# Weighing the values of two query tiles in one run of TensorE

## What is computed

```python
def attention(h, wq, wk, wv, wo):
    q = (h @ wq).reshape(b, s, NH, D).transpose(0, 2, 1, 3)
    k = (h @ wk).reshape(b, s, NKV, D).transpose(0, 2, 1, 3)
    v = (h @ wv).reshape(b, s, NKV, D).transpose(0, 2, 1, 3)
    k = jnp.repeat(k, GROUPS, axis=1)
    v = jnp.repeat(v, GROUPS, axis=1)
    scores = jnp.einsum('bhqd,bhkd->bhqk', q, k) / jnp.sqrt(jnp.float32(D))
    scores = jnp.where(causal, scores, jnp.finfo(scores.dtype).min)
    attn = jax.nn.softmax(scores, axis=-1)
    out = jnp.einsum('bhqk,bhkd->bhqd', attn, v)
    return out.transpose(0, 2, 1, 3).reshape(b, s, NH * D) @ wo
```

## Time and profile before

| | us |
|---|---|
| three runs: lowest, median, highest | 1846.94, 1847.69, 1847.88 |
| the profiled execution, own time | 1847.24 |
| its span, first to last instruction | 1845.5 |
| busy in the span: PE, PE's weight loads | 1745.3, 1388.8 |
| busy in the span: ACT, DVE, POOL | 1061.6, 1037.0, 208.0 |
| first and last record of the runs of line 1300 | 223.9, 1343.1 |

### The profile page before, as it was taken

How to read it: one execution, slowest core, us unless ns; L and a number is a source line. 1 busy time by engine, 2 the same in 40 slices (tenths; PEclk the granted TensorE clock), 3 DMA queues, 4 the chain that set the end, 5 groups by cost and what they waited for, 6 DMA issues and landing times.

```text
span 1845.5 us, 31643 instructions
## 1 busy us (share of the span) xinstructions
PE 1745.3 (95%) x12158; PEld 1388.8 (75%) x12158; DVE 1037.0 (56%) x2595; ACT 1061.6 (58%) x2377; POOL 208.0 (11%) x236
## 2 busy tenths in 40 slices
PE   5999699999999999999999999999958999999993
PEld 4777377777777777777777777777748999999993
DVE  3677586686686677676776776766752111111112
ACT  3444487787777777777877777777731222222223
POOL 2222100000000000000000000000002222222222
PEclk9999799999999999999999999999968999999997
DMA  3000100000000000000000000000034153113443
GB/s 86 2 2 2 46 1 10 1 1 10 1 1 9 1 1 9 1 1 9 1 1 9 1 1 1 1 1 23 1 135 163 28 159 91 24 28 91 146 106 97
DMA packets 46054, 60.19 MB, mean 33 GB/s; under 512 B 8944, under 2 KB 39536, under 8 KB 45936
## 3 DMA queue, kind: packets, MB, share of 16 engines
q1 hardware_dynamic: 36336, 46.16, 7.5%
q0 software_dynamic: 7536, 10.36, 3.4%
q10 hardware_dynamic: 2064, 2.10, 0.4%
HBM read 138.43 MB, written 11.40 MB: 81 GB/s over the span
## 4 chain that ended last, share of the span: by engine, by line
PE 93%; DVE 3%; ACT 1%; POOL 1%; DMA 1%; issue 0%; SPq 0%; POOLq 0%; DVEq 0%
PE wide L1388 15%; PE bank L1300 14%; PE bank L1288 14%; PE bank L1245 9%; PE wide L1277 9%; PE wide L1278 8%; PE bank L1397 7%; PE bank L1309 6%; PE bank L1108 3%; PE wide L1120 1%; PE bank L1190 1%; PE bank L1179 1%; PE bank L1133 1%; PE bank L1235 1%; PE wide L1349 1%; PE bank L1102 1%
## 5 line engine op out<-in xcount | busy, mean ns | idle before, releaser
L886 DVE CUSTOM_DVE_ANT_0 arena<-wide,arena 128x896 f32<-128x896 f32 (+7 forms) x512 | 383.1, 756 | 243.0 <-PE wide L1278 236.7
L655 ACT ACTIVATE arena<-arena,nmax 128x896 f32<-128x896 f32 (+7 forms) x512 | 399.1, 780 | 89.8 <-DVE nmax L886 87.6
L662 ACT COPY arena<-bank 128x512 f32<-128x512 f32 x576 | 311.7, 586 | 82.7 <-PE bank L1288 77.2
L1277 PE MATMUL wide<-khi,qhl 128*128 128x512 f32 (+3 forms) x768 | 344.4, 450 | 1.7 <-DVE qhl L879 1.7
L1288 PE MATMUL bank<-ident,arena 128*128 128x128 f32 x2304 | 309.5, 274 | 2.5 <-DVE arena L894 1.2
L1388 PEld LDWEIGHTS wide<-wo,arena 128*128 128x128 f32 x2496 | 284.8, 192 | 3.1 <-issue 1.1
L1388 PE MATMUL wide<-wo,arena 128*128 128x128 f32 x2496 | 285.1, 275 | 0.9 <-ACT wo L710 0.9
L1288 PEld LDWEIGHTS bank<-ident,arena 128*128 128x128 f32 x2304 | 260.0, 141 | 29.3 <-issue 14.1
L1300 PE MATMUL bank<-arena,vt 128*64 128x256 f32 x2304 | 277.0, 385 | 0.0
L894 DVE TENSOR_SCALAR arena<-arena,rinv 128x896 f32<-128x896 f32 (+7 forms) x512 | 258.2, 525 | 9.1
L1049 DVE TENSOR_TENSOR wo<-wide,wo 128x512 f32<-128x512 f32 x78 | 53.9, 692 | 365.7 <-PE wide L1388 365.7
(11 more groups left out here) (221 smaller groups left out, 1576.4 us busy)
## 6 DMA issues: line engine op xcount, KB each, us to landing
arena<-in_L_ffn_w SPq DMA_DIRECT2D x117, 1024.0 KB
x_all<-in_L_attn_x ACTq DMA_DIRECT2D x1, 2048.0 KB, 9.9
wq_g<-in_L_ffn_wq SPq DMA_DIRECT2D x8, 256.0 KB, 3.0
wo<-in_L_ffn_wo SPq DMA_DIRECT2D x16, 128.0 KB, 3.0
hbuf<-acc SPq DMA_DIRECT2D x2, 1024.0 KB, 4.5
tbuf<-rT_all SPq DMA_DIRECT2D x4, 512.0 KB, 3.0
acc<-hbuf SPq DMA_DIRECT2D x4, 512.0 KB, 5.8
out<-x_all SPq DMA_DIRECT2D x8, 256.0 KB, 2.1
```

Source lines behind the costliest of these rows:

```text
L655: nc.scalar.activation(probs[t % 2][:, h, 0:w], probs[t % 2][:, h, 0:w], ACT.Exp, bias=nmax[:, t % 2, h:h + 1], scale=-1.0, accum_out=rsum ...
L662: nc.scalar.copy(pT[t % 2][m], bank_of((t, m))).then_inc(S("pT_ready"), 1)
L886: nc.vector.tensor_tensor_reduce(out=probs[t % 2][:, h, 0:w], in0=score_bank(t, h)[:, 0:w], in1=causal[:, SEQ - w:SEQ], scale=-1.0, scalar ...
L1277: mm(dst, q, khi[:, lo:lo + cols], start=True, stop=False)
```

## The change

PE weighs two tiles in one run in the even steps: in step t the tiles t - 3 and t - 2, each into its own half of `bank[2]` (512 columns now). In the next, odd step both outputs are projected right behind S0, into one of the three shared banks, for which `("O", s)` joins the list of turns, ahead of the step's blocks. ACT copies both tiles at once into an `oT` of twice the size. DVE adds both at once in the odd step, between maximum 1 and maximum 2 (in two instructions where the tiles belong to two sequences). `acc_done` counts those adds, and the loop has two more steps at its end.

```diff
+def weighed_in(t):
+    return [x for x in (t - 3, t - 2) if 0 <= x < TILES] if t % 2 == 0 else []
+def added(t):
+    return sum(len({x // TB for x in weighed_in(s) if x <= t}) for s in range(2, t + 4, 2))
+STEPS = TILES + 4
+def turns_of(t):
+    turning = 1 <= t <= TILES
+    blocks = [[(t - 1, m) for m in third(t - 1, p)] if turning else [] for p in range(3)]
+    out = [("O", t - 1)] if weighed_in(t - 1) else []
+    item = [item_of(t)] if t < TILES and item_of(t) else []
+    return out + blocks[0] + blocks[1] + blocks[2] + item
+TURNS = FIRST_ITEMS + [x for t in range(STEPS) for x in turns_of(t)]
...
-        oT = sb("oT", [P, 2, P])
+        oT = sb("oT", [P, 2, 2, P])
...
-            sp.wait_ge(S("acc_done"), BATCH * NKV * TB - TB)
+            sp.wait_ge(S("acc_done"), added(TILES - TB - 1))
...
-                if weighing:
-                    act.wait_ge(S("o2_psum"), t - 1)
-                    nc.scalar.copy(oT[:], bank[2][:, 0:2 * P].rearrange("p (j c) -> p j c", j=2)).then_inc(S("oT_ready"), 1)
+                if weighed_in(t):
+                    n = 2 * P * len(weighed_in(t))
+                    act.wait_ge(S("o2_psum"), t // 2)
+                    nc.scalar.copy(oT[:].rearrange("p x j c -> p (x j c)")[:, 0:n], bank[2][:, 0:n]).then_inc(S("oT_ready"), 1)
...
                 if scored:
                     maximum(t, 1)
+                if weighed_in(t - 1):
+                    tiles = weighed_in(t - 1)
+                    v.wait_ge(S("proj2"), (t - 1) // 2)
+                    new = bank_of(("O", t - 1))[:, 0:D * len(tiles)].rearrange("p (x d) -> p x d", d=D)
+                    for n in sorted({x // TB for x in tiles}):
+                        xs_ = [x for x in tiles if x // TB == n]
+                        at, lo = xs_[0] % (BATCH * TB), tiles.index(xs_[0])
+                        old = acc[:, at:at + len(xs_)]
+                        nc.vector.tensor_tensor(old, new[:, lo:lo + len(xs_)], old, ALU.add).then_inc(S("acc_done"), 1)
                 if scored:
                     maximum(t, 2)
                     normalise(t, 0)
-                if weighing:
-                    n, ct = divmod(t - 2, TB)
-                    v.wait_ge(S("proj2"), t - 1)
-                    at = acc[:, n % BATCH * TB + ct]
-                    nc.vector.tensor_tensor(at, bank[2][:, 2 * P:2 * P + D], at, ALU.add).then_inc(S("acc_done"), 1)
...
                     before = TURNS[TURN_OF[what] - 3]
                     if len(before) == 3:
                         wait_taken(before)
+                    elif before[0] == "O":
+                        pe.wait_ge(S("acc_done"), added(weighed_in(before[1])[-1]))
                     else:
                         pe.wait_ge(S("pT_ready"), blocks_before(before[0]) + before[1] + 1)
...
-            def values(t):
-                n, ct = divmod(t, TB)
-                if t:
-                    pe.wait_ge(S("acc_done"), t)
-                for m in range(ct + 1):
+            def values(s):
+                if s > 2:
+                    pe.wait_ge(S("oT_ready"), s // 2 - 1)
+                for x, t in enumerate(weighed_in(s)):
+                    n, ct = divmod(t, TB)
+                    for m in range(ct + 1):
...
-            def project_out(t):
+            def project_out(s):
+                wait_bank(("O", s))
+                to = bank_of(("O", s))
...
+                pe.wait_ge(S("oT_ready"), s // 2)
+                for x, t in enumerate(weighed_in(s)):
+                    for j in range(2):
+                        ins = mm(to[:, x * D:(x + 1) * D], oT[:, x, j], wo2[:, t // (BATCH * TB), j], start=(j == 0), stop=(j == 1))
...
-                if weighing:
-                    values(t - 2)
+                if weighed_in(t):
+                    values(t)
+                if weighed_in(t - 1):
+                    project_out(t - 1)
...
-                if weighing:
-                    project_out(t - 2)
```

More of the change, by code:

```diff
@@ L73, in third @@
     return range(blocks * p // 3, blocks * (p + 1) // 3)
-FIRST_ITEMS = [(0, 0, 0), (0, 1, 0), (0, 2, 0), (0, "V", 0)]
-TURNS = FIRST_ITEMS + [x for t in range(TILES + 1)
-                       for x in ([(t - 1, m) for p in range(3) for m in third(t - 1, p)] if t else []) + ([item_of(t)] if t < TILES and item_of(t) else [])]
+def weighed_in(t):
[3 more added lines that the diff above has]
+STEPS = TILES + 4
+FIRST_ITEMS = [(0, 0, 0), (0, 1, 0), (0, 2, 0), (0, "V", 0)]
+def turns_of(t):
[5 more added lines that the diff above has]
+TURNS = FIRST_ITEMS + [x for t in range(STEPS) for x in turns_of(t)]
 TURN_OF = {x: i for i, x in enumerate(TURNS)}
@@ L363, in _ @@
             t_v = tbuf.rearrange("(t p) d -> p t d", p=P)
-            sp.wait_ge(S("acc_done"), BATCH * NKV * TB - TB)
+            sp.wait_ge(S("acc_done"), added(TILES - TB - 1))
             sp.dma_start(h_v[:, 0:TB], acc[:, 0:TB]).then_inc(S("h_stored"), 16)
-            sp.wait_ge(S("acc_done"), BATCH * NKV * TB)
+            sp.wait_ge(S("acc_done"), added(TILES - 1))
             sp.dma_start(h_v[:, TB:NT], acc[:, TB:NT]).then_inc(S("h_stored"), 16)
@@ L667, in _ @@
                 evacuate(item)
-            for t in range(TILES + 2):
-                scored, turning, weighing = t < TILES, 1 <= t <= TILES, t >= 2
+            for t in range(STEPS):
+                scored, turning = t < TILES, 1 <= t <= TILES
                 if t and t <= TILES and item_of(t - 1):
@@ L688, in _ @@
                     exponent(t, 3)
-            act.wait_ge(S("acc_done"), BATCH * NKV * TB)
+            act.wait_ge(S("acc_done"), added(TILES - 1))
             for t in range(NT // 4):
@@ L925, in _ @@
                     normalise(t, 1)
-            v.wait_ge(S("acc_done"), BATCH * NKV * TB)
+            v.wait_ge(S("acc_done"), added(TILES - 1))
             for t in range(NT // 4):
@@ L1289, in turn_part @@
                     ins.then_inc(S("pT_psum"), 1)
-            def values(t):
-                n, ct = divmod(t, TB)
-                if t:
-                    pe.wait_ge(S("acc_done"), t)
-                for m in range(ct + 1):
[L1296 to L1301, removed]
+            def values(s):
[4 more added lines that the diff above has]
+                    for m in range(ct + 1):
+                        pe.wait_ge(S("pT_ready"), blocks_before(t) + m + 1)
+                        if m == ct and ct % (TB // 2) == 0:
+                            pe.wait_ge(S("v2_ready"), 2 * n + 1 + ct // (TB // 2))
+                        for u in range(2):
+                            ins = mm(bank[2][u * DH:(u + 1) * DH, x * 2 * P:(x + 1) * 2 * P], vt[:, n % 2, m], pT[t % 2][m][:, u * 2 * P:(u + 1) * 2 * P],
+                                     start=(m == 0), stop=(m == ct))
                 ins.then_inc(S("o2_psum"), 1)
-            def project_out(t):
-                if t == 0:
+            def project_out(s):
+                wait_bank(("O", s))
+                to = bank_of(("O", s))
+                if s == 2:
                     pe.wait_ge(S("wo2_loaded"), 16 * 2 * NKV)
-                pe.wait_ge(S("oT_ready"), t + 1)
-                for j in range(2):
-                    ins = mm(bank[2][:, 2 * P:2 * P + D], oT[:, j], wo2[:, t // (BATCH * TB), j], start=(j == 0), stop=(j == 1))
+                pe.wait_ge(S("oT_ready"), s // 2)
+                for x, t in enumerate(weighed_in(s)):
+                    for j in range(2):
+                        ins = mm(to[:, x * D:(x + 1) * D], oT[:, x, j], wo2[:, t // (BATCH * TB), j], start=(j == 0), stop=(j == 1))
                 ins.then_inc(S("proj2"), 1)
@@ L1335, in _ @@
                     project(item_of(t))
-            pe.wait_ge(S("acc_done"), BATCH * NKV * TB)
+            pe.wait_ge(S("acc_done"), added(TILES - 1))
             for t in range(NT // 4):
```

## The result

The changed kernel takes **1872.91 us** (median of four runs, 1872.56 to 1875.33), beside 1847.79 for the kernel before in the same comparison: 1.0135 times as long, interval 1.0122 to 1.0148. The forecast was 1875 in a range of 1860 to 1888, slower with a chance of 0.87. The profiled execution is the longest of the four, 1875.33 with a span of 1873.3.

A forecast was written before the change was run, and what follows sets the result against it. PE's in-order work was taken to bound the kernel. Fewer runs (-22.0), old waits gone (-15.5) and new waits (+65) make +27.5 us on the profiled 1847.24, forecast 1875, range 1860 to 1888.

The forecast's parts named there:

- Fewer runs, -22.0: PE's weighing: 128 runs become 65, each of the 63 saved worth 0.35 us beyond its blocks, -22.0 us.
- The cost goes with the form of the weights: On PE, a run's 0.35 us comes from 64-column weights in place of 128, not from the change of data type.
- rival C: Any full-precision matmul between scores costs the 0.35, so odd steps' output projections cancel the saving: 1897 us, 5 in 100.
- The waits that come, +65: Short odd steps and step 0 of eight: PE waits for DVE and ACT, 4.29 us per sequence, +65 us.
- 1.4 and 0.9 that went: Per sequence of eight tiles, the forecast period loses 1.4 us for fewer runs and 0.9 for present waits.
- the walk: Instruction-by-instruction timing of odd steps on PE, DVE and ACT; the last of each eight waits 2.15 us, ending at 10.12.
- the restart: On PE, a turned block that waited for DVE ends 0.77 us after DVE's end, against 0.44 alone.
- The joined add: On DVE, one add over 512 columns takes 0.69 us, like a copy; 0.84 would give 7 us more at most.
- The ends: Fifteen sequences have the new waits, 64 us, the last lacks most of them; 1 us is added for the loop's ends.
- three bounds: Margins on the sum: add 7 us more, restarts 5 less, entry into output projection 4 more; range 1868 to 1884.
- Rivals A and B: New waits overlap, 1825 to 1810 us (7 in 100); or b1 and b2 hardly wait, 1844 to 1851 (5 in 100).
- 37 us of savings: On PE over the whole loop: -22.0 us from fewer runs and -15.5 us from present waits that go.

The follow-up runs named there:

- e1: Kernel before, each weighing run of two or more blocks cut in two, second half behind the second head's score (240 runs, not 128): 1879.73 us, ratio 1.0162.
- e2: Changed kernel, with the output projection written into bank[2] instead of taking a turn of the shared banks: 1853.71 us, ratio 1.0023.
- e7: e2, with DVE making the item's low part behind maximum 1 in the last step of each eight: 1849.12 us, ratio 1.0007.
- e3: Changed kernel, each tile weighed in its own step again (128 runs), output, copy and add still paired, shared bank kept: 1867.01 us, ratio 1.0091.
- e6: e2, with single-tile runs in steps 7 and 0 of eight, pairs in 2, 4, 6 (81 runs), output projection moved: 1835.48 us, ratio 0.9934.
- e9: e6, with the item projected ahead of the turned block in step 1 of each eight: 1821.45 us, ratio 0.986.
- e4: Changed kernel with parities swapped, pairs weighed in odd steps and outputs projected in even ones: 1895.62 us, ratio 1.0252.

## Why the prediction was right

*Fewer runs, -22.0.* The size held: the trace has the 65 runs, a run has 0.15 in front, and a score of 512 columns behind it takes 0.43, in the new trace as in the old. Where that score is shorter it takes less (0.26 in ct 0), but again 0.20 more than the next one. e1 pays 0.35 per added run where a score follows and 0.30 where a block does.

*The cost goes with the form of the weights.* O between S0 and S1 leaves the next score as short as ever, so rival C is out. But 64 columns are not the whole of it: X, whose weights have 64 rows and 128 columns, also stands ahead of a score that takes 0.43 (here in ct 3), as it did before the change. So the price seems to come with any change of the form of the weights, which no run tests by itself.

```profile
741.22 0.39 PE bank L1263 x4
741.61 0.43 PE wide L1305
```

The Trainium skill's rule that a change of the tiling mode drains the engine (TensorEngine Tiling (Array Packing), Key Properties) fits what the rows show, and they give the size that it lacks: 0.15 going in, 0.15 to 0.20 coming out.

*The waits that come, +65.* The mechanism and its places were right, each with its releaser; the size was a tenth too large for a sequence. With the 1.4 and 0.9 that went, a period of 72.28 leaves 3.87 of new waits instead of 4.29. In ct 7 DVE was where the walk had it to 0.02: low part done 4.07 behind S0 (forecast 4.09), the add 5.95 (5.96). What was too long was the restart. The block behind the add ends 0.71 after it, not 0.77, and X ends 0.50 behind the copy of b4, not 0.64; X thus ends at 9.89 instead of 10.12. The 0.77 was read at a block that had waited for a normalisation. In ct 3 and ct 5 the restart is as short:

```profile
739.84 0.68 DVE acc L945 x2
...
740.56 0.66 PE bank L1316 x4
...
754.71 0.61 DVE acc L945
...
755.37 0.66 PE bank L1316 x4
```

The block ends 0.71 behind the add. There DVE is through a little earlier too: the add ends 4.42 behind S0 in ct 3 (forecast 4.50) and 4.19 in ct 5 (4.32), since neighbouring instructions on DVE overlap by up to 0.09 in the records at more places than the walk had allowed for.

*The joined add.* I took 0.69 from a copy of the same size; by form the trace now has

```profile
L945 DVE TENSOR_TENSOR acc<-bank,acc 128x512 f32<-128x512 f32 x48 | 32.8, 682 | 7.4 <-PE bank L1342 7.4
```

0.682, so the lower end was right and the 7 us for 0.84 fall away. (They were 4.5 at most: a block waits behind the joined add in ct 5 and ct 7 alone, 30 times and not 45.)

*The ends.* Of the 24.9 by which the loop ends later, the 14 sequences between the first and the last make 22.1, 1.58 each. I had counted the first like those, at +2.0; from its S0 to the next sequence's it took 61.53 instead of 62.70, 1.2 less, and began 0.6 later. And I had let the last save 2.3, without new waits; from its S0 to the loop's end it took 82.54 instead of 79.18, 3.4 more. That step of the prediction failed: the waits come in the last sequence too, whose first seven steps alone grew by 1.6, like those of the others. Beside the forecast the last sequence is 5.7 over, the first 2.6 under, and the 14 between 5.7 under. So the sum, +27.5 against +24.9 for the loop, is closer than its parts, and that is luck; without the last sequence's miss the kernel would take some 1867, which lies in the range too.

*The range.* The three bounds that I named (7 and 4 more, 5 less) make 1870 to 1886 and not the 1868 to 1884 that I wrote. The result lies in both. In ct 7, the pieces of PE's own work as listed make 7.99, not 7.96; its end at 10.12 doesn't rest on that.

*Rivals A and B* needed the waits to be under about 2.6 a sequence. They are 3.87, and e2, with 2.54 of new waits (70.95 less 68.41), shows what B would have looked like: 1853.71 beside 1850.04.

So where did 37 us of savings go? PE did its work in the order in which it is written, as the chains show, and an odd step's V and O had a second use: they filled the time in which DVE went through a maximum, two normalisations, the low part and another maximum. Moved to the even step, PE's work was done as quickly, but ct 3, 5 and 7 were then as long as DVE's and ACT's chain. Of that loss the banks taken by O make about 20 us (e2) and the order of the low part 4 (e7), and putting V back wins more than it costs (e3). By its chain, what keeps ct 7 long in e7 is O ahead of S1, with low part and add ahead of maximum 2. e6 and e9 leave ct 7 its own run and put O further down, and ct 7 has its old 11.45 again; which of the two does it isn't shown.

## What to carry to other kernels

Before work is moved off a step of an in-order queue, ask what other engine's chain it covers there: a saving on the bounding engine counts only where no wait stands behind it, and too long a run ahead of the first result that others need can cost as much as too short a one (e4). Joining work of two iterations pays if each step keeps enough to cover the chain, and if what is joined takes no buffer out of a rotation; here pairs in three of eight steps, with O in the run's own bank and the item first in ct 1, gave -1.4%, and pairs in four of eight, with O in the rotation, +1.35%.

## What the runs showed of the hardware

- Leaving the 64-column form costs 0.20 before a score of 512 columns in fp32r and 0.15 before a transposed block of 128 columns (e1). I had one figure for both. A score behind X, which has 64 rows of weights, pays 0.20 as well.
- A block that waited for DVE's add ended 0.71 after it, 0.27 more than the 0.44 of such a block in a row; behind the normalisation it was 0.77.
- An add of 512 fp32 columns with one operand in PSUM took 682 ns, a copy of that size 692: the second operand cost nothing.
- The granted clock stayed at 1.00 through a loop in which PE idled for about 2 us in every 72, never longer than 0.71 at a time in the steady part.
